# Linear attention in sub-chunks of 64 tokens, on quarter tiles of TensorE, with one scan for the states and new engine orders

## What is computed

```python
Q = phi(x @ Wq); K = phi(x @ Wk); V = x @ Wv        # phi(x) = elu(x) + 1
S = cumsum(K[t] outer V[t]); z = cumsum(K[t])       # over the tokens t, per head
out = (Q[t] . S[t]) / max(Q[t] . z[t], 1e-6)
x = x + concat(out) @ Wo
h = layernorm(x); x = x + gelu(h @ Wf1) @ Wf2
```

## Time and profile before

| | us |
|---|---|
| median of 3 runs (707.84 to 708.77) | 708.24 |
| the profiled execution | 708.78 |
| its span, first to last instruction | 707.0 |
| PE, DVE, ACT, POOL busy | 670.2, 529.6, 432.2, 246.1 |
| DMA, mean | 57 GB/s |

### The profile page before, as it was taken

One profiled execution on the slowest core, in us unless ns is written; L12 is line 12 of the kernel. 1 busy time (PEld: TensorE's weight loads), 2 busy tenths in 40 slices (PEclk: granted clock), 3 DMA queues, 4 the chain that ended last, 5 costly groups with the idle time before them and its releaser, 6 DMA issues.

```text
span 707.0 us, 23400 instructions
## 1 busy us (share of the span) xinstructions
PE 670.2 (95%) x9378; PEld 572.9 (81%) x9378; DVE 529.6 (75%) x1565; ACT 432.2 (61%) x846; POOL 246.1 (35%) x271
## 2 busy tenths in 40 slices
PE   3899999999999999999999999999988999999995
PEld 2678888888888788888888888888767989999983
DVE  4867787787878778877878787698686687655674
ACT  4565576558466855766585568546644666666646
POOL 6200013025312411331243025114213657765664
PEclk9999999999999999999999999999999999999998
DMA  7330010001000100100010001001021223345446
GB/s 247 112 59 14 3 32 17 17 19 47 31 9 12 52 27 14 51 17 17 18 47 17 18 18 32 17 10 36 7 76 48 69 77 128 108 136 149 137 153 182
DMA packets 46522, 40.29 MB, mean 57 GB/s; under 512 B 9104, under 2 KB 41232, under 8 KB 46416
## 3 DMA queue, kind: packets, MB, share of 16 engines
q1 hardware_dynamic: 35360, 25.25, 12.9%
q0 software_dynamic: 4784, 10.39, 4.3%
q10 hardware_dynamic: 6272, 3.16, 1.5%
HBM read 23.12 MB, written 15.66 MB: 55 GB/s over the span
## 4 chain that ended last, share of the span: by engine, by line
PE 76%; DVE 12%; ACT 8%; issue 2%; DMA 1%; DVEq 0%; ACTq 0%
PE banks_o L718 9%; PE banks_sc L561 8%; PE banks_o L542 6%; PE bank_u L446 5%; PE banks_o L552 4%; PE bank_u L535 4%; PE bank_q L434 3%; PE bank_q L436 3%; PE bank_q L435 3%; DVE work L1252 2%; PE bank_k L434 2%; PE banks_sc L446 2%; PE bank_k L436 2%; PE bank_k L435 2%; PE banks_sc L434 2%
## 5 line engine op out<-in xcount | busy, mean ns | idle before, releaser
L1718 POOL DMA_INDIRECT routed_rows<-routed,slot x64 | 63.2, 988 | 151.8 <-PE banks_sc L561 120.4
L823 ACT ACTIVATE work<-bank_u 128x512 f32<-128x512 f32 x64 | 38.3, 599 | 115.1 <-PE bank_u L446 115.1
L1268 DVE TENSOR_TENSOR work<-banks_sc,causal 128x1024 f32<-128x1024 f32 x64 | 77.8, 1216 | 1.4 <-PE banks_sc L561 0.3
L718 PE MATMUL banks_o<-w,work 128*128 x624 | 76.2, 275 | 0.0
L561 PE MATMUL banks_sc<-work 64*64 64x128 f32 x2048 | 70.2, 274 | 5.5 <-ACT v_aug L823 0.8
L718 PEld LDWEIGHTS banks_o<-w,work 128*128 128x128 f32 x624 | 72.9, 192 | 0.3 <-issue 0.2
L542 PE MATMUL banks_o<-v_aug,work 128*64 128x65 f32 x2048 | 71.5, 223 | 0.0
L1252 DVE SCALAR_TENSOR_TENSOR work<-bank_q,work 128x512 f32<-128x512 f32 x64 | 43.7, 683 | 36.3 <-ACT work L887 36.0
L1686 POOL TENSOR_SCALAR ve<-mv 128x4 f32<-128x4 f32 x24 | 4.7, 196 | 178.8 <-DVE mv L1134 178.6
L542 PEld LDWEIGHTS banks_o<-v_aug,work 128*64 128x64 f32 x2048 | 66.1, 139 | 0.0
L561 PEld LDWEIGHTS banks_sc<-work 64*64 64x64 f32 x2048 | 56.8, 133 | 11.1 <-issue 9.9
(11 more groups left out here) (322 smaller groups left out, 1792.3 us busy)
## 6 DMA issues: line engine op xcount, KB each, us to landing
work<-in_L_attn_x SPq DMA_DIRECT2D x16, 256.0 KB, 3.4
work<-routed_rows SPq DMA_DIRECT2D x20, 132.0 KB, 2.1
xg_more<-routed_rows SPq DMA_DIRECT2D x19, 132.0 KB, 2.2
stage<-in_L_ffn_w SPq DMA_DIRECT2D x8, 256.0 KB, 2.7
moe_input<-routed SPq DMA_DIRECT2D x8, 256.0 KB, 2.2
work<-moe_input ACTq DMA_DIRECT2D x8, 256.0 KB
v_aug<-expert_results SPq DMA_DIRECT2D x4, 512.0 KB, 6.9
out<-work SPq DMA_DIRECT2D x6, 256.0 KB, 2.8
```

The source lines that it names most:

```text
L718: mm = pe.matmul(Y[t % 2][:, blk(k)], hTe[t % 2][:, f, blk(k)], w2[:, bass.ds(e[t] * F + f * D, D)], start=(f == 0), stop=(f == NF - 1))
L1268: dve.tensor_tensor(am_all, sc_banks.rearrange("p (x s) -> p x s", s=P), causal[:, :].unsqueeze(1).broadcast_to([P, 2 * CH, P]), ALU.mult) ...
L1718: pool.indirect_dma_start(rows_d, bass.IndirectOffsetOnAxis(slot[:, k, c:c + 1], 0), routed[:, c, k, :], None).then_inc(sct, 16)
```

## The change

Chunks of 128 tokens become eight sub-chunks of 64 (`SUB`, `NS`). A score product then has 64 columns instead of 128 and fills a 64 x 64 block; the mask is one block `causal_sub`, repeated (4 chunks, 2 heads: 512 elements a partition). Sub-chunk 2c + r lies with its tokens on partitions 64r to 64r + 63 of chunk c, so the products of masked scores and values (`inner`) and those for the states (`own_column`) contract over 64 rows: all of them are quarter tiles. There are seven states instead of three, so 14 own products and 14 across products a step in place of 6 and 12; inner stays at 16, scores at 16. The own products are written with a step of seven elements, so that one scan of DVE (state = link * state + own, where `link` is 0 at the start of each run of seven and 1 elsewhere) makes all states:

```diff
-                for c in range(CH - 1):
-                    u = bkC[:, c * DV1:(c + 1) * DV1]
-                    if c == 0:
-                        ins = dve.tensor_copy(state[:, 0, :], u)
-                    else:
-                        ins = dve.tensor_tensor(state[:, c, :], u, state[:, c - 1, :], ALU.add)
...
+                dve.tensor_tensor_scan(state[:, :], link[:, :], bkC[:, 0:DV1 * (NS - 1)], 0.0, ALU.mult, ALU.add
+                                       ).then_inc(s_sb, 1)
```

```diff
+            columns = bkC[:, 0:DV1 * (NS - 1)].rearrange("p (v j) -> p v j", j=NS - 1)
+
+            def own_column(g, c, r, h):
+                return pe.matmul(columns[HEADS[h], :, 2 * c + r], ktok[HEADS[r], c, HEADS[h]],
+                                 va[HEADS[r], c, 2 * (g % PAIRS) + h, :], start=True, stop=True)
+
+            def inner(g, c, r, h, first=False):
+                rows, cols_ = place_of(2 * c + r)
+                return pe.matmul((bkG, bkH)[h][rows, cols_], am[g % 2][HEADS[r], h, c, :],
+                          va[HEADS[r], c, 2 * (g % PAIRS) + h, :], start=first, stop=False)
...
+                for pair in ((1, 2), (4, 3), (5, 6), (7,)):
+                    for j in pair:
+                        rows, cols_ = place_of(j)
                         for h, hs in enumerate(HEADS):
-                            mm = pe.matmul((bkG, bkH)[h][rows, blk(c, DV1)], qT[cur][hs, blk(2 * c + n, DH)],
-                                           state[hs, c - 1, :], start=False, stop=(c == CH - 1))
+                            mm = pe.matmul((bkG, bkH)[h][rows, cols_], qT[cur][hs, blk(j, SUB)], states_by[hs, :, j - 1],
+                                           start=False, stop=(j in (5, 7)))
```

```diff
+                def k_next():
+                    if nxt:
+                        pe.wait_ge(a_msk, g + 1)
+                        k_proj(npar, np_)
...
+                elif p == 3 and not last:
+                    b_free(g - 1)
+                    front_t(b + 1)
+                    second_half(g - 1)
+                    pe.wait_ge(h32_sb, b + 2)
+                    scores(g)
...
+                elif p == 3:
+                    q_next()
+                    across_last()
+                    k_next()
+                    v_next()
+                    h2_t(b - 1, bkC)
+                    wo_two_back()
+                    otr_last()
+                    pe.wait_ge(h232_sb, b)
+                    keys_t(g)
+                    a_free(g)
+                    ffn1(b - 1, 0, bkA)
```

More of the change, by code:

```diff
@@ L490, in ffn1, with ffn2 @@
                 split3(out[:, :], wf1, blk(f), h2T, ALLT).then_inc(ff1_mm, 1)
-            def ffn2(b, out):
-                for f in range(NF):
+            def ffn2(b, out, fs):
+                for f in fs:
                     pe.wait_ge(g_lo, b * NF + f + 1)
@@ L578, in step @@
                 npar, np_ = (g + 1) // PAIRS % 2, (g + 1) % PAIRS
-                if g > 0:
-                    columns(g - 1)
-                    if p == 2 and not first:
-                        a_free(g - 1)
-                        y_t(b - 1, bkA)
-                    if p == 3 and not last:
-                        b_free(g - 1)
-                        front_t(b + 1)
-                    across(g - 1)
-                pe.wait_ge(q_phi, g + 1)
-                pe.wait_ge(k_phi, g + 1)
-                pe.wait_ge(v_sb, min(CH + g, 2 * CH * B))
@@ L619, in step @@
-                if p in (5, 6):
-                    wo_acc(g - 2)
-                if nxt:
-                    if p == 3 and not last:
-                        pe.wait_ge(h32_sb, b + 2)
-                    b_read = {5: [(s3_sb, b)], 6: [(x3T_sb, b)]}.get(p, [])
-                    for what, count in b_read:
-                        if not first:
-                            pe.wait_ge(what, count)
-                    k_proj(npar, np_)
-                if g == 2:
-                    pe.wait_ge(wof_lo, 1)
@@ L645, in step @@
[L645 to L666 removed]
+                    if nxt:
+                        q_proj(npar, np_)
@@ L903, in step @@
                 nxt = g + 1 < B * PAIRS
+                if p == 3 and not last:
+                    front_scale(b + 1, True)
+                    front_high(b + 1, 1 - b % 2)
                 if not first:
@@ L922, in step @@
                     scale2(b - 1, bkC)
-                if nxt:
-                    q_exps(g + 1)
-                if p == 3 and not first:
                     h2_copy(b - 1)
-                if nxt:
-                    k_exps(g + 1)
+                late_keys = p == 3 and not first or p in (6, 7)
+                if not late_keys:
+                    ktok_copy(g)
+                if p == 2:
+                    w1_high(b)
                 if p < CH:
@@ L1335, in step, with normalise_last, q_next, k_next @@
+                def normalise_last():
+                    if g > 0:
+                        normalise(g - 1)
+                def q_next():
+                    if nxt:
+                        q_phis(g + 1, (g + 1) % 2)
+                def k_next():
+                    if nxt:
+                        k_phis(g + 1, (g + 1) % 2)
+                def mask_here():
+                    mask(g)
+                    if last and p >= CH:
                         for t in (2 * (p - CH), 2 * (p - CH) + 1):
@@ L1351, in step @@
-                if p == 4 and first:
-                    w1_low(b)
-                if p == 5 and first:
-                    front_stats(2)
-                if p == 1 and not last:
-                    front_apply(b + 1)
-                if nxt:
-                    q_phis(g + 1, (g + 1) % 2)
-                if p == 3 and not first:
-                    low2(b - 1)
-                if nxt:
-                    k_phis(g + 1, (g + 1) % 2)
-                if p == 3 and not last:
-                    front_low(b + 1, 1 - b % 2)
```

464 lines of the change are left out of this document (294 added, 170 removed).

## The result

The changed kernel takes **717.65 us** (median of 4 runs, 715.63 to 719.14) where the kernel before took 708.18 on the same chip (707.84 to 708.77): ratio 1.0131, 95% interval 1.0102 to 1.016. Slower by 1.3%, where 685 us were forecast. The profiled execution took 715.63 us, its span is 713.8.

The account below looks back on a forecast made before the run. PE was taken to bound the kernel (95% busy, 76% of the chain). Profiled 708.8 us, less 36 saved in 64 steps, plus 12.6 of new waits, gave 685.4, forecast as 685; range 660 to 712.

Parts of the forecast that it names:

- I take 16 because L552 has the very tile and length: PE's new quarter-tile blocks: each record priced at 16 ns, as in the old across group; ends 13.5 and 32.
- changes of form: PE switching between tile forms around the across block: 0.12 us in and 0.19 out, perhaps 0.1 for the next projection.
- milder half: Only the PSUM writes or only the reads double in price: 704 us; a third of the chance of 0.19.
- Rival 2: Own-column and across records, at a step of seven, take double, 32 ns: kernel slower, 728 us; chance 0.19.
- (b): p=3: PE waits ahead of ffn1, its input queued on ACT behind q_exps and k_exps: 1.2 us lost per sequence.
- (c): p=7: otr waits for normalise, which stands behind logits and top2: 0.3 us lost per sequence.
- saving of 0.56 a step: PE per step: 3.08 us removed, 2.52 added; 36 us saved in 64 steps.
- VectorE's terms: Mask falls from 1216 to 691 ns; three state operations, 0.67 us, become a scan of 1.10; 0.1 less a step.
- rival 3: DVE becomes the bound; seven sequences lose 0.5 us in each of five special steps: 702 us; chance 0.15.
- (a): p=3: scores wait until ACT has read front_t's result from bank_k: 0.5 us lost per sequence.
- w1's lower halves on POOL: Eight lower halves of w1 move from DVE to mostly idle POOL: priced at nothing.
- Rival 4: Mixed row groups make tiles wait for each other, records at 26.6 ns: 746 us; chance 0.04.

Follow-up runs that it names:

- e1: Changed kernel, but across products read 65 adjacent state words instead of words seven apart (other values multiplied): 0.9998 of the kernel before.
- t1: Changed kernel with only the across reads made adjacent, one of four runs on one slower chip: 1.0001 of the kernel before.
- t0: The changed kernel itself, unedited, first of four runs on one slower chip: 1.0275 of the kernel before.
- b7: Kernel before with its three states kept seven fp32 words apart instead of side by side: 1.0148 of the kernel before.
- b4: Kernel before with its three states kept four fp32 words apart instead of side by side: 1.0157 of the kernel before.
- e2: Changed kernel with adjacent across reads and own columns also written side by side in PSUM (other values): 0.9989 of the kernel before.
- h2: Changed kernel with p=3's earlier order and seven dependent VectorE operations on adjacent columns in place of the scan: 1.0251 of the kernel before.
- t2: Changed kernel with only p=3's order of work put back as in the kernel before, same chip as the change's rerun: 1.0096 of the kernel before.
- t3: Changed kernel with both adjacent across reads and p=3's earlier order, same chip as the change's rerun: 0.9829 of the kernel before.
- b2: Kernel before with its three states kept two fp32 words apart instead of side by side: 0.9987 of the kernel before.
- k1: Changed kernel with p=3's earlier order; TensorE adds neighbouring own columns, VectorE makes states by one copy and three sums: 702.47 us, 0.9912 of the kernel before.

## Why the prediction was wrong, by its own steps

**Failed: "I take 16 because L552 has the very tile and length", for the across records.** The sum gave them 28*16 = 0.45 us a step, and the block 0.76 with its changes of form. The block measured 1.10, its records 32 ns apart, against 0.63 with adjacent reads (e1). So the step of seven in the reads costs 0.47 us a step, 30 us in 64 steps, where the sum had nothing for it; against the block's own term the miss is 0.34, since the changes of form were priced 0.13 too dear. The cause is shown by e1 against the change and by t1 against t0, where only the reads differ; b7 and b4 show the same records at 297 to 298 ns in the kernel before.

685.4 + 30 = 715.4, and the profiled execution took 715.63. That closeness is in part luck, for the steps do not close one by one: with the dear reads the terms give 7.56 us for p=1 and 7.55 for p=5, and 7.12 and 7.25 were measured; they give 28.6 for p=2 to p=4 together, and 29.25 were measured.

The text named the danger and gave its milder half a third of 0.19. Rival 2 was the outcome, on the reading side only, and its price of 704 was too low. It took off 10 us for time that would fall into waits (b) and (c). Wait (b) is as long with cheap reads as with dear ones (10.6 and 10.1 us), so nothing was to be taken off for it; for (c) it was some 0.37 us a sequence, 3 us in all. Without the deduction the price is 714.

**Right: the record price elsewhere.** Inner and own-column records start 16 ns apart and the scores take 0.47. With adjacent reads the plain step is 6.40 us (t1), the forecast to the hundredth; so the saving of 0.56 a step is there. The whole sequence agrees as well: sequence 1 of t1 takes 62.4 us, 62.6 forecast. In PSUM the step of seven cost nothing: 224 ns in e1 with it, 222 in e2 without. The Trainium skill (PSUM — Partial Sum Buffer, Specifications) says that a non-contiguous pattern in PSUM slows matmuls significantly; for these quarter-tile fp32 products the trace doesn't agree. The prediction's rival held both sides, PSUM and SBUF, and the rule spoke for the side that did no harm.

**Right: VectorE's terms.** Mask 686 ns (691 forecast). The scan of 455 elements took 1095 ns (1.10 forecast, the upper bound). Less the fixed 0.16 us that the prediction's rows give (225 - 65*1.04), that is 2.06 ns an element, against 1.04 of other operations. The Trainium skill (DVE: opcode table, instruction layouts, handler registers and perf-mode slots, Datapath and trigger behaviour) has the built-in scan at half throughput, and the row agrees. VectorE did not become the bound in the change (72% busy, 8% of the chain); rival 3 did not come. h2 shows that it was near: half a microsecond more a step, and PE waits in 50 of them.

**Right in kind, roughly in size: the waits.** (a) 0.25 ahead of the scores of p=3, 0.5 forecast. (b) 1.31 ahead of ffn1, 1.2 forecast. (c) 0.3 at p=7: with dear reads the across block hides it; with cheap ones p=7 gains 0.10 where plain steps gain 0.47, so some 0.37 is waited there. Together 12.6 us were forecast for (a), (b) and (c), and the order of p=3, which takes away (a) and (b), gives back 13 (t2); the steps of the eight sequences show 12 of them.

**No cost seen** of w1's lower halves on POOL (36% busy), though no run isolates it. Rival 4 did not come either: records 16 ns apart show that the tiles run side by side.

The range, 660 to 712, held rival 2's milder half only at the price with the deduction; the full price, 714, lies outside it.

**Open.** On the chips where the kernel before takes 735 to 741 us, the change loses another 1.4% by late signals at p=1 to 3; whether they hang on its order of work was not tried. Without both causes the kernel is at 0.983 there, not at the 0.949 (708.8 - 36 = 672.8) of the forecast without waits: some 25 us. A later sequence of t3 takes 3.6 to 3.8 us more than its sequence 1, and the kernel before has some 1.4 of the kind (b2); over six sequences that is about 14. Sequence 1 of t3, at 61.3 us, is 0.5 above the forecast without waits (62.6 - 1.8 = 60.8), some 4 us in eight. The rest is not assigned.

## What to carry to other kernels

When an edit changes in which order an operand lies in memory, price every reader of it again, even if tile and length stay: 65 fp32 values read seven words apart took the distance of TensorE's records from 18 to 32 ns here. Here the scan wanted its seven steps side by side and the matmul its 65 columns; k1 got adjacent reads without the scan, by letting TensorE add neighbours in PSUM. Where a step slows two engines at once, as in b7, ask of each whether something covers it: there the slower VectorE operations cost more of a plain step than the slower matmuls. And an engine that is busy 20% less than the bound need not have room: 31 us more on VectorE cost 29.

## What the runs showed of the hardware

- A quarter-tile fp32 record of 65 columns lasts 224 to 227 ns with its moving operand in SBUF side by side or two words apart, and 297 to 298 ns at four or seven; the distance of records goes from about 18 ns (e1, (0.70-0.224)/27) to 32 in the change, and from 15.4 to 27 in the kernel before (b7, (0.92-0.298)/23). A write to PSUM at a step of seven costs none of this (224 ns in e1, 222 without the step in e2).
- A VectorE operation that makes such a row by adding 65 columns takes 225 to 226 ns side by side or at two words, and 276 to 277 at four or seven.
- The same kernel before took 708.2, 708.5, 735.4, 739.0, 739.9 and 740.9 us on the chips of this study (the mean granted clock of the profiled runs was 0.99 to 1.00 on the two fast chips and 0.97 to 0.99 on the others), and the change stood at 1.013 of it on the first and at 1.0265 and 1.0275 on two of the others. A ratio of 1% is to be trusted on its own chip only.
- On the chips of 735 us and more, some VectorE operations at p=1 to p=3 wait 1.2 to 2.2 us, from sequence 2 on, for a release of which the trace has no record (t0, t1, t3); sequence 5 of the change is 3.0 us longer than on the first chip, and one of the kernel before some 1.4 (b2). Sequence 1 there, and all on the first chip, have no such wait.
